# A loop of fifteen iterations with one round each, written as five iterations with three rounds each

## The reference, cut to what matters

```python
xn = layernorm(x)
s = attn0(xn)            # 4 inner layers: LN, q k v, two Hamilton products, a spectral filter, projection, LN, MLP 128->512->128
g = silu(experts0(xn))   # 8 experts, top 2, hidden width 256
x = x + s * g
xn = layernorm(x)
s = attn1(xn)            # 16 heads of 64, windows of 128 looking one window back, rotary
g = silu(experts1(xn))   # 32 experts of width 64, top 4 in 2 of 4 groups, and a shared one
x = x + s * g
```

## Time and profile before

| | |
|---|---|
| median of 3 runs | 4673.15 us (4673.07 to 4688.22) |
| the profiled execution's own time | 4671.39 us |
| its span, from the first to the last instruction | 4669.6 us |
| mean granted TensorE clock | 0.956 of full speed |
| busy | PE 90%, PE weight loads 56%, DVE 80%, ACT 69%, POOL 44% |
| chain that ended last | PE 40%, DVE 22%, "issue" 21%, POOL 8%, ACT 6% |

### The profile page before, as it was taken

The page is one execution under the profiler, slowest core; times in us unless marked ns, Lnnn a source line. Parts: engine busy times, 40 slices in busy tenths (PEclk is TensorE's granted clock), DMA queues, the critical chain, the costliest instruction groups (busy, mean ns, idle before and its releaser), DMA issues.

```text
span 4669.6 us, 75535 instructions
## 1 busy us (share of the span) xinstructions
PE 4215.7 (90%) x20080; PEld 2591.7 (56%) x20208; DVE 3738.3 (80%) x8946; ACT 3231.8 (69%) x6125; POOL 2055.7 (44%) x2033
## 2 busy tenths in 40 slices
PE   5669999898998989999898998989999898999979
PEld 3336556565565656555565665656556565655655
DVE  4779798787978879798787978879798887979843
ACT  2447777676776767777676777767777676777745
POOL 1235455444444444454444534544444444445523
PEclk8779999999999999999999999999999999999979
DMA  4011111011111111111111111101111111111100
GB/s 130 14 28 27 30 32 35 26 31 32 29 27 32 35 27 32 29 30 32 29 31 33 27 27 33 36 23 31 33 30 28 31 33 30 27 29 32 35 21 21
DMA packets 144533, 149.42 MB, mean 32 GB/s; under 512 B 27748, under 2 KB 107932, under 8 KB 143960
## 3 DMA queue, kind: packets, MB, share of 16 engines
q1 hardware_dynamic: 144088, 144.19, 11.9%
HBM read 22.45 MB, written 4.19 MB: 6 GB/s over the span
## 4 chain that ended last, share of the span: by engine, by line
PE 40%; DVE 22%; issue 21%; POOL 8%; ACT 6%; SPq 1%; DVEq 1%; DMA 0%; POOLq 0%; ACTq 0%
DVE acc L952 5%; PE bT L1326 5%; PE bU L1364 5%; DVE tmp L952 4%; PE bA L1174 4%; PE bG L1357 4%; PE bC L1371 4%; PE bA L1264 3%; PE bT L1158 3%; POOL s_h L644 3%; DVE nmax L1100 3%; PE bA L1255 2%; PE bT L1284 2%; DVE hu L1139 2%; PE bT L1339 2%
## 5 line engine op out<-in xcount | busy, mean ns | idle before, releaser
L644 POOL TENSOR_TENSOR s_h<-s_h,ge 128x512 f32<-128x512 f32 x512 | 712.6, 1392 | 1184.1 <-ACT ge L654 954.4
L952 DVE TENSOR_TENSOR tmp<-comps 128x512 f32<-128x512 f32 x768 | 585.1, 768 | 8.9
L1371 PE MATMUL bC<-hu,w_d 128*128 128x512 f32 x1056 | 572.3, 624 | 8.7 <-DVE hu L1139 8.2
L776 ACT ACTIVATE s_h<-bG 128x512 f32<-128x512 f32 x528 | 314.8, 596 | 376.9 <-PE bG L1357 208.5
L952 DVE TENSOR_TENSOR acc<-acc,tmp 128x512 f32<-128x512 f32 x768 | 567.3, 740 | 8.0
L753 ACT ACTIVATE probs<-bT,nmax 128x256 f32<-128x256 f32 x1024 | 408.1, 474 | 185.9 <-DVE nmax L1100 183.5
L1139 DVE TENSOR_TENSOR hu<-bU,s_h 128x512 f32<-128x512 f32 x528 | 362.3, 686 | 173.9 <-POOL s_h L644 103.8
L631 POOL TENSOR_TENSOR rot<-rot,sinT 128x512 f32<-128x512 f32 x256 | 355.2, 1388 | 303.5 <-DMA rot<-raw 303.5
L1326 PEld LDWEIGHTS bT<-V,probsT 128*128 128x128 f32 x3584 | 430.8, 193 | 80.6 <-issue 37.1
L622 POOL TENSOR_TENSOR comps<-comps 128x255 f32<-128x255 f32 (+1 forms) x384 | 298.0, 776 | 379.5 <-ACT comps L700 379.4
L1326 PE MATMUL bT<-V,probsT 128*128 128x65 f32 x3584 | 442.0, 276 | 13.4 <-ACT probsT L654 12.2
(11 more groups left out here) (201 smaller groups left out, 9392.8 us busy)
## 6 DMA issues: line engine op xcount, KB each, us to landing
rot<-raw SPq DMA_DIRECT2D x1024, 64.0 KB, 2.0
comps<-comps SPq DMA_DIRECT2D x384, 120.0 KB
x_ld<-in_L_attn_x SPq DMA_DIRECT2D x66, 128.0 KB, 2.2
comps<-comps SPq DMA_DIRECT2D x384, 8.0 KB
out<-O SPq DMA_DIRECT2D x16, 256.0 KB, 2.9
w_a<-in_L_attn_W_qkv SPq DMA_DIRECT2D x1, 1536.0 KB, 14.5
w_fc<-in_L_attn_fc_w SPq DMA_DIRECT2D x1, 1024.0 KB, 7.9
w_g<-in_L_ffn_w_gate SPq DMA_DIRECT2D x1, 1024.0 KB, 6.0
```

The costliest lines, as they stand in the source:

```text
L644: nc.gpsimd.tensor_tensor(s_h[:, :], s_h[:, :], ge[:, :], ALU.mult).then_inc(weighed, 1)
L776: nc.scalar.activation(s_h[:, :], bG[:, :], ACT.Silu).then_inc(silu, 1)
L952: V_.tensor_tensor(dst, i0, i1, op).then_inc(ham[h], 1)
L1371: ins = mm(bC[:, :], down, hu[:, :], start=u in (0, UNITS0), stop=u in (UNITS0 - 1, UNITS - 1))
```

## The change: what it does

```diff
+UNROLL = 3
...
         def rounds(eng, one):
 
             one(first)
-            with eng.Fori(1, NB) as i:
-                one(middle(i))
+            with eng.Fori(0, (NB - 1) // UNROLL) as i:
+                for k in range(1, UNROLL + 1):
+                    one(middle(i * UNROLL + k))
             one(last)
```

## The result

| | before | after |
|---|---|---|
| median | 4675.48 us (4 runs) | 4647.41 us (4 runs, 4644.22 to 4651.74) |
| ratio | | 0.9935, 95% interval 0.9921 to 0.9949 |
| measured once more (6 runs, 11 of before) | 4673.78 us | 4650.92 us, ratio 0.9949 (0.9936 to 0.9962) |
| span of the profiled execution | 4669.6 us | 4646.5 us |

The kernel is faster by 30 us by the first ratio and by 24 us by the second (28 and 23 us by the medians), some two thirds of the 41 us that were forecast. The first median lies inside the range by 0.6 us, the second above it by 2.9 us: that the time fell inside is in part luck.

The account below looks back on a forecast made before the run. No engine is full; time is lost at taken branches, with DVE's hole on the chain. Ten seams at 4.09 us give 40.9 us, all other terms zero: 4671.39 - 40.9 = 4630.5, plus 1.8, forecast 4632 us, range 4620 to 4648.

Parts of the forecast that it names:

- DVE's hole: DVE's issue wait at the statistics behind a taken branch, 2.66 us each, on the chain; 14 fall to 4.
- the entry: Loop entered from the written-out first round without a taken branch; its round takes 274.21 us against 278.30 for the others.
- Each seam is worth 4.09 us: Ten back edges that become plain continuations save 278.30 - 274.21 = 4.09 us each, 40.9 us in all.
- the clock behind the seam: TensorE's low clock after a seam: 6.8 us behind a back edge, 3.5 us behind the entry; worth 1.4 us.
- The bound of 32 us: Gain from the ten seams if a straight round ran 0.9 us longer than the one sample.
- PE's hole: PE's wait at a round's first gate matmul, 2.22 us each; not on the chain by itself, closing it lengthens a later wait.
- Rival A: Only DVE's hole goes, the low clock behind each seam stays as long: 27 us gained, 4646 us; chance 0.11.
- Table load: ACT's load of 1.28 us goes at ten seams; worth zero, 13 us at most if its cover were gone.
- register instructions: Two to eight fewer per engine and iteration; below 2.5 us, taken as zero.
- POOL and SP at zero: POOL's block fetch at a seam is covered by 19.5 us, SP's x load isn't awaited until late: both worth zero.
- Rival C: Slower: POOL's longer code no longer stays loaded, 42 fetches cost up to 112 us, 4744 us; chance 0.03.
- rival B: The holes close and nothing comes of it, a taken branch costing only its own 63 ns: 4672 us; chance 0.08.

Follow-up runs that it names:

- the hint: Kernel before, still fifteen iterations, with each engine's first instruction in the loop a hint that the back edge will be taken: 4643.03 us, ratio 0.9927.
- DVE alone: Against the kernel before, only DVE has three rounds per iteration, the other engines keep 15 iterations: 4637.83 us, ratio 0.9914.
- the fifteen-fold loop: All fifteen rounds written out in one iteration on all engines (`UNROLL = 15`), against the kernel before: 4641.74 us, ratio 0.9929.
- fifteen rounds with two fills: All fifteen rounds written out on all engines, plus six unused matmuls at each seam and four ahead of a round's first scores: 4618.20 us, ratio 0.9876.

## Why the prediction was right, and where it was too large

*DVE's hole lies on the chain, 14 go to 4, and the fetch is what it is made of.* Right. The seam got 2.74 us shorter exactly as at the entry, the hint took the hole away without a longer body, and DVE alone brought the whole gain.

*Each seam is worth 4.09 us.* This is the term that was mis-sized: it measured 278.30 - 275.69 = 2.61 us in the changed kernel. It rested on one round, the first of the loop, which happened to have the clock low for only 6.8 us in all. Straight rounds average 11.3, rounds of before 14.4. The part of it that belongs to the seam was foretold well: 6.8 us at the low level behind a branch and 3.5 behind a plain seam were read from two stretches, and the means are 7.6 and 3.1; at the first scores matmul the entry was ahead by 3.50 us and the straight rounds by 3.44. But the prediction put all that goes beyond the hole, 1.4 us, down to the clock behind the seam. Up to the scores it is 0.7; the entry's round gained the other 0.6 later, and the straight rounds lost 0.8 there, where they have some 1.3 us more at the low level than rounds of before. That this sample was no mean is seen from the same round in other kernels without a fill: 274.2 to 277.7 us. The bound of 32 us, for straight rounds 0.9 us longer, was nearer than the value taken.

*PE's hole costs nothing by itself, and closing it only lengthens PE's second wait.* Right as to the chain: PE alone unrolled wins nothing. What the prediction didn't see is that a kernel that leaves PE's branch in place does better: 3.81 us a seam (278.30 - 274.49) and 40 us by the ratio with DVE alone, which is the forecast's size by a road that it did not describe. This isn't why the 4.09 were too many: the entry's round, from which they come, has PE's idle time in one piece too (2.8 us), and the same fall behind it.

*Rival A (only the hole goes, 4646 us)* had the time and the mean round (275.6 foretold, 275.69 measured), but not its mechanism: the low stretch behind the seam did get shorter, and what that won was given back later in the round. So the kernel's time alone can't tell the two apart.

*Table load, register instructions, POOL and SP at zero.* Right within what can be measured: 255 table loads, all register instructions gone in the fifteen-fold loop without a gain, POOL and SP kept short with the same time. The table loads were not tried by themselves; the kernel with the hint keeps all 265 and wins as much. Rival C is refuted by the kernel with POOL and SP kept short, rival B by the measured gain and by the hint.

*What stays open:* why straight rounds have more time at the low clock later on, by which they lose what the entry's round kept; why kernels that leave PE's branch in place are faster; why fifteen rounds with two fills are no faster than three; and why some seams keep the full clock while like ones beside them don't.

## What to carry to other kernels

A taken branch can cost far more than its own duration, here 2.7 us on DVE. It counted only on the engine that is waited for at the seam, and there a hint or a longer body on that engine alone removed it. When a wait is removed, look at how the idle time of TensorE lies afterwards, and what the clock does behind it: unused matmuls in the gap won as much as the change. Take the worth of a step from many rounds, and a profile's rounds with the distance of its execution from the median; one round that happens to be in the trace carries its own luck with the clock.

## What the runs showed of the hardware

- The price of a taken branch stands at the branch on PE (3.3 to 3.7 us median) and behind it on DVE (63 ns at the branch, 2.6 us until the next instruction).
- A hint at the top of the body removed it on DVE (0.38 us left; body of 902 instructions) and not on PE (3630 ns; body of 1029 as the program is built).
- Adding 2.9 us of TensorE work a round, where it stood idle, made the kernel 0.6% faster before the change and 0.6 to 0.7% after it, and took the fall of the granted clock away from most seams.
